# Cross-attention layer, four times in sequence: split-weight places from five to four, ring places from eleven to twelve, and a new table of the order of steps

## The reference, cut to what matters

```python
H = 1024; NH = 32; KVH = 8; HD = 32; GROUPS = 4; EPS = 1e-06     # 8 batches, L = S = 512
q = hidden_state @ Wq + bq                       # 512 x 1024
k = encoder_hidden_state @ Wk + bk               # 512 x 256
v = encoder_hidden_state @ Wv + bv               # 512 x 256
scores = jnp.einsum('bkgld,bksd->bkgls', q, k) * scale
scores = scores + encoder_attention_mask[:, :, None, :, :]
attn = jax.nn.softmax(scores, axis=-1)
out = jnp.einsum('bkgls,bksd->bkgld', attn, v)
out = out.transpose(0, 3, 1, 2, 4).reshape(b, l, H)
out = out @ Wo + bo
x = out + hidden_state                           # then a layer norm over H, times gamma, plus beta
```

## Time and profile before

| | before |
|---|---|
| median of 3 runs | 1693.84 us |
| the profiled execution, its own time | 1699.61 us |
| its span, first to last instruction | 1697.8 us |
| mean granted TensorE clock | 0.979 |
| busy: PE / DVE / ACT / POOL | 94% / 85% / 81% / 55% |
| share of the chain that ended last: PE / DVE / ACT | 68% / 8% / 4% |
| HBM over the span | 194 GB/s |

### The profile page before, as it was taken

One profiled execution on the slowest core, in us unless ns is written; L12 is line 12 of the kernel. 1 busy time (PEld: TensorE's weight loads), 2 busy tenths in 40 slices (PEclk: granted clock), 3 DMA queues, 4 the chain that ended last, 5 costly groups with the idle time before them and its releaser, 6 DMA issues.

```text
span 1697.8 us, 38272 instructions
## 1 busy us (share of the span) xinstructions
PE 1594.9 (94%) x14048; PEld 1107.2 (65%) x14048; DVE 1447.2 (85%) x2773; ACT 1370.9 (81%) x3186; POOL 936.6 (55%) x731
## 2 busy tenths in 40 slices
PE   4798899999999999999999999999999999999986
PEld 3565566666667666676676675777666676667654
DVE  4578899889888988899888898888988899887986
ACT  4678788869888788878988789887898879887794
POOL 5335433437745458544766357653585536856383
PEclk9899999999999999999999999999999999999998
DMA  9878787558895589756887668865898548894332
GB/s 201 233 207 213 203 215 202 158 132 184 251 249 131 149 198 272 222 146 154 213 265 186 165 155 211 277 170 146 196 241 255 156 130 206 270 277 126 98 99 106
DMA packets 357435, 325.54 MB, mean 192 GB/s; under 512 B 145792, under 2 KB 248192, under 8 KB 357248
## 3 DMA queue, kind: packets, MB, share of 16 engines
q1 hardware_dynamic: 353472, 322.55, 71.4%
q10 hardware_dynamic: 3776, 0.54, 0.3%
HBM read 245.38 MB, written 83.89 MB: 194 GB/s over the span
## 4 chain that ended last, share of the span: by engine, by line
PE 68%; DVE 8%; ACT 4%; issue 3%; DMA 1%; SPq 0%; POOL 0%; DVEq 0%; ACTq 0%
PE bank L1881 38%; PE bank L1962 13%; PE bank L1942 10%; DVE probs L1768 3%; DVE turned_p L1784 3%; PE bank L1977 3%; ACT probs L1666 2%; PE bank L2002 1%; PE bank L1990 1%; PE bank L1918 1%; DMA w_raw<-in_L_xattn_Wo_dram 1%; DVE ring_raw L1731 1%; ACT pv_sb L1679 0%; ACT y_sb L1690 0%; ACT part L1656 0%
## 5 line engine op out<-in xcount | busy, mean ns | idle before, releaser
L1881 PE MATMUL bank<-ring_hi,w_sb 128*128 128x512 f32 x2368 | 793.3, 400 | 29.0 <-issue 19.4
L1666 ACT ACTIVATE probs<-probs,shift 128x512 f32<-128x512 f32 x1024 | 729.4, 717 | 55.7 <-DVE shift L1768 54.4
L1768 DVE CUSTOM_DVE_ANT_0 probs<-bank,mask_l 128x512 f32<-128x512 f32 x1024 | 652.6, 677 | 105.7 <-PE bank L1942 97.4
L1784 DVE STREAM_TRANSPOSE turned_p<-probs 128x2048 f32<-128x2048 f32 x256 | 588.3, 2301 | 63.8 <-ACT probs L1666 62.1
L1551 POOL TENSOR_TENSOR w_sb<-w_raw,w_sb 128x512 fp32r<-128x512 f32 x320 | 413.4, 1298 | 384.9 <-ACT w_sb L1623 384.8
L1881 PEld LDWEIGHTS bank<-ring_hi,w_sb 128*128 128x128 f32 x2368 | 446.7, 190 | 154.8 <-issue 47.6
L1881 PE MATMUL bank<-ring_lo,w_sb 128*128 128x512 f32 x1184 | 469.4, 396 | 0.0
L1942 PE MATMUL bank<-k_stack,q_stack 96*128 96x512 f32 x1024 | 346.6, 415 | 24.5 <-DVE shift L1768 17.8
L1962 PE MATMUL bank<-turned_p,v_all 32*32 32x512 f32 x8192 | 294.7, 614 | 13.1 <-issue 7.5
L1566 POOL TENSOR_TENSOR ring_lo<-ring_raw,ring_hi 128x512 fp32r<-128x512 f32 x168 | 215.3, 1292 | 127.4 <-ACT ring_hi L1635 126.9
L1942 PEld LDWEIGHTS bank<-k_stack,q_stack 96*128 96x128 f32 x1024 | 189.2, 191 | 142.5 <-DVE shift L1768 55.9
(11 more groups left out here) (75 smaller groups left out, 963.2 us busy)
## 6 DMA issues: line engine op xcount, KB each, us to landing
w_raw<-w_d SPq DMA_DIRECT2D x144, 256.0 KB, 4.2
q_stack<-q_hi_d SPq DMA_DIRECT2D x128, 256.0 KB, 4.6
w_raw<-in_L_xattn_Wo_dram SPq DMA_DIRECT2D x128, 256.0 KB, 3.2
q_hi_d<-part_hi SPq DMA_DIRECT2D x64, 256.0 KB, 3.4
q_lo_d<-part SPq DMA_DIRECT2D x64, 256.0 KB, 3.9
q_stack<-q_lo_d SPq DMA_DIRECT2D x64, 256.0 KB, 4.2
v_all<-v_d SPq DMA_DIRECT2D x256, 64.0 KB, 2.7
out_dram<-y_sb SPq DMA_DIRECT2D x32, 512.0 KB, 4.5
```

The costliest lines, as they stand in the source:

```text
L1666: nc.scalar.activation(probs[:, st % 2, h, :], probs[:, st % 2, h, :], ACT.Exp, scale=-1.0, bias=shift[:, g % 2, i:i + 1], accum_out=sums[ ...
L1768: nc.vector.tensor_tensor_reduce(out=probs[:, st % 2, h, :], in0=S_ps[h][:, :], in1=mask_l[:, lb, :], scale=-1.0, scalar=HIGHEST, op0=ALU. ...
L1784: nc.vector.transpose(turned_p[:, :, block_of(g, st) + g % 2, :, :].rearrange("p j h c -> p h j c"), probs[:, st % 2, :, :].rearrange("p h ...
L1881: mm = nc.tensor.matmul(C[c][:, :], w_sb[:, n_w, (1, 0, 0)[third], d % 4, :], (hi, lo, hi)[third], start=(n == 0), stop=(n == 23))
```

## The change

`SLOTS`, the ring's places, goes from 11 to 12, and `NW`, the places for split weights, from 5 to 4. A place of either kind takes 4 KB of a partition, so memory stays as it is. `BASE` and all of `PLACES` have new numbers; the kinds and the number of the steps, `WINDOWS` and every instruction stay. A program's row of the diff shows what such numbers look like, and says nothing more:

```diff
-BASE = {1: 242.38, 2: 449.20, 3: 658.37, 4: 866.32, 5: 1074.27, 6: 1282.22, 7: 1490.17}
+BASE = {1: 232.33, 2: 435.46, 3: 639.46, 4: 840.58, 5: 1043.23, 6: 1245.48, 7: 1448.77}
...
-        "w_load Q": (
-            (13.583, 17.803),
+        "w_load Q": (
+            (23.287, 24.722),
...
-    SLOTS = 11
-
-    NW = 5
+    SLOTS = 12
+
+    NW = 4
```

More of the change, by code:

```diff
@@ new lines @@
+        "stack": (52.701, 77.364, 82.777, 111.918, 118.414, 153.577, 168.308, 197.908),
+        "recip": (86.598, 105.703, 129.112, 161.423, 171.071, 205.345, 215.721, 243.462),
+        "spread": (82.601, 115.511, 130.837, 160.246, 188.712, 222.964, 233.336, 240.415),
+        "v_load": (77.927, 82.788, 99.049, 124.782, 134.392, 160.941, 198.988, 210.865),
+        "pv": (84.915, 104.601, 128.361, 152.454, 175.118, 206.271, 223.447, 242.512),
+        "sel": (98.413, 118.866, 138.384, 164.408, 188.823, 215.945, 232.746, 255.261),
@@ new lines @@
+        "stack": (-7.624, -1.643, 26.536, 48.796, 68.761, 99.923, 131.304, 151.496),
+        "recip": (31.518, 47.625, 78.796, 102.726, 128.085, 158.252, 186.293, 206.818),
+        "spread": (35.422, 57.631, 80.693, 113.542, 132.238, 160.887, 189.330, 227.207),
+        "v_load": (-6.866, 9.124, 38.540, 99.912, 118.772, 121.624, 132.067, 163.237),
+        "pv": (31.884, 54.240, 81.788, 108.642, 131.388, 158.071, 184.939, 214.112),
+        "sel": (41.978, 61.293, 93.426, 117.760, 142.342, 175.628, 196.607, 229.196),
@@ L335 @@
-            (124.600, 131.861),
-            (138.176, 141.865),
+            (121.440, 121.769),
+            (129.232, 131.315),
+            (133.504, 137.115),
+            (138.870, 139.649),
         ),
         "w_hi kv": (
-            (123.172, 126.717),
-            (128.039, 132.341),
-            (141.477, 141.695),
-            (142.923, 150.012),
+            (125.884, 131.312),
+            (139.404, 142.699),
+            (147.408, 149.127),
+            (149.973, 154.490),
         ),
@@ L455 @@
+            (115.128, 119.290),
         ),
         "w_lo o": (
[L457 to L468 removed]
@@ L469 @@
-        "y_turn o": (69.641, 75.364, 94.730, 98.243, 102.980, 121.031, 126.326, 147.526),
-        "y_add o": (69.834, 70.418, 95.831, 98.791, 105.535, 124.055, 125.542, 149.802),
+            (56.103, 58.322),
+            (59.365, 62.524),
+            (63.590, 67.809),
+            (68.275, 73.344),
+            (81.980, 94.906),
+            (96.311, 107.880),
+            (108.672, 113.553),
+            (114.829, 123.368),
+        ),
+        "keep o": (67.524, 69.082, 75.621, 99.384, 101.983, 108.629, 124.682, 129.382),
@@ L483 @@
+        "z o": (163.862, 172.267, 180.578, 192.550),
+        "zmul o": (168.287, 174.416, 182.202, 198.021),
+        "zadd o": (168.400, 175.129, 191.825, 202.615),
+        "z_store o": (179.416, 196.150, 203.685, 210.336),
+        "root o": 157.335,
+        "rstd o": 159.813,
     },
@@ new lines @@
+        "stack": (-8.336, 12.458, 29.717, 48.201, 71.870, 99.130, 113.984, 165.901),
+        "recip": (32.055, 55.672, 87.023, 107.441, 131.672, 167.705, 188.555, 220.575),
+        "spread": (35.468, 52.659, 88.011, 106.475, 136.216, 171.661, 189.595, 226.047),
+        "v_load": (-11.038, 30.571, 56.573, 87.481, 97.941, 145.501, 150.413, 179.039),
+        "pv": (31.314, 51.805, 83.449, 109.798, 131.278, 159.868, 184.703, 217.027),
+        "sel": (40.991, 61.440, 91.326, 117.961, 142.787, 175.534, 202.280, 226.585),
@@ L700 @@
-        "y_turn o": (67.814, 76.014, 96.223, 99.263, 104.986, 125.290, 127.080, 147.928),
-        "y_add o": (67.751, 69.246, 96.593, 99.064, 104.062, 124.045, 126.255, 148.109),
+            (50.720, 52.659),
+            (63.201, 76.127),
+            (79.797, 83.364),
+            (84.540, 85.279),
+            (88.523, 89.046),
+            (94.919, 100.495),
+            (107.440, 108.925),
+            (115.712, 116.664),
+        ),
+        "keep o": (71.408, 74.815, 76.133, 88.157, 97.863, 104.962, 121.056, 129.109),
@@ L708 @@
-        "z o": (172.873, 174.156, 174.775, 181.954),
-        "zmul o": (180.075, 193.586, 196.132, 198.965),
-        "zadd o": (185.089, 199.833, 201.121, 212.459),
-        "z_store o": (195.130, 201.181, 205.726, 209.124),
-        "root o": 153.734,
-        "rstd o": 161.794,
+            (99.471, 103.601, 106.177, 109.064),
+            (152.681, 152.712, 154.416, 155.452),
+        ),
+        "res o": (19.516, 20.556, 34.801, 53.288),
+        "aggr o": (153.070, 155.944, 157.095, 157.232),
@@ L714 @@
+        "z o": (165.910, 173.278, 180.557, 193.182),
+        "zmul o": (169.868, 186.701, 188.100, 190.943),
+        "zadd o": (171.650, 188.474, 189.367, 203.143),
+        "z_store o": (176.211, 200.761, 206.660, 212.066),
+        "root o": 155.121,
+        "rstd o": 159.130,
     },
@@ L775 @@
-        "mask": (-15.884, -7.281, -1.566, -5.584),
[14 rows of a table removed]
-        ),
[2 rows of a table removed]
+            (36.333, 38.783, 40.181, 40.535),
+            (58.235, 58.582, 59.105, 60.390),
+            (87.341, 87.402, 90.312, 90.542),
+            (114.186, 115.176, 115.359, 115.389),
+            (135.630, 136.361, 137.599, 138.063),
+            (159.723, 160.270, 160.898, 161.291),
+            (182.621, 183.316, 184.498, 185.911),
+            (203.286, 205.977, 205.685, 205.735),
+        ),
+        "stack": (-9.716, 8.560, 30.313, 41.352, 75.159, 94.372, 138.733, 141.082),
@@ new lines @@
+        "recip": (26.017, 63.312, 86.147, 105.943, 125.853, 156.708, 178.007, 205.222),
+        "spread": (38.334, 61.960, 81.443, 100.607, 138.390, 166.349, 186.619, 195.931),
+        "v_load": (-12.772, 34.437, 50.974, 60.484, 94.383, 113.150, 170.071, 172.668),
+        "pv": (31.381, 53.330, 82.635, 112.499, 135.319, 155.228, 180.899, 199.826),
+        "sel": (42.923, 63.000, 96.248, 117.675, 139.040, 162.018, 187.127, 207.588),
+        "rbc": (44.097, 71.493, 96.419, 119.729, 139.116, 166.942, 189.235, 199.700),
@@ L927 @@
-        "res e": (-30.114, -26.465, 57.137, 57.836),
-        "z_store e": (219.999, 228.652, 229.634, 231.634),
[2 rows of a table added]
+        ),
+        "res o": (20.546, 24.885, 25.463, 64.595),
+        "aggr o": (148.017, 149.121, 148.558, 149.531),
+        "z o": (159.671, 165.117, 170.255, 177.028),
+        "zmul o": (157.017, 169.980, 175.510, 182.031),
+        "zadd o": (166.338, 170.524, 190.077, 205.623),
+        "z_store o": (177.515, 187.740, 197.414, 210.689),
+        "root o": 150.317,
+        "rstd o": 156.708,
```

675 lines of the change are left out of this document (305 added, 370 removed), and 556 rows, old and new, of the table PLACES.

## The result

| | before | changed |
|---|---|---|
| median | 1694.91 us (4 runs, 1692.93 to 1697.62) | 1676.09 us (4 runs, 1673.66 to 1678.15) |
| ratio | 1 | 0.9884, 95% interval 0.9864 to 0.9904 |
| the profiled execution, its own time / span | 1699.61 / 1697.8 us | 1676.28 / 1673.9 us |
| mean granted TensorE clock | 0.979 | 0.986 |

The account below looks back on a forecast made before the run. PE, busy 94% of the span, was taken as the bound, so only waits could change: -5.0 - 1.5 - 4.5 + 1.0 + 2.8 = -7.2 us, from 1693.8 to 1686.6 us. Its own range was 1680 to 1692, the whole range 1667 to 1706.

Parts of the forecast that it names:

- The square root in group 5: Batches 2 to 6, PE's wait after pv of group 5: copies 0.3 us earlier each, -1.5 us; bounds -11 and +4.
- Batches 2 and 4: ACT's queue no longer stopped by a late o0 weight transfer, so they fall to the others' time: -5.0 us.
- Prologue and batch 0: Prologue +1.0 us (weight cover, first scores); batch 0 -4.5 us: stack wait of group 1 -2.5, wait before its pv -2.0.
- Four places in the steady batches: Four weight places instead of five: refills stay covered while landing is under 7.5 us, cost 0.
- End: Row blocks and last pv: refills with four places come late, 1.4 to 1.5 and 1.3 us, together +2.8 us.
- Slower, places too few: Rival: one tight half in each of batches 1 to 6 meets a late landing, 1704.2 us; chance 0.22.
- Nothing comes of it: Rival: the waits trade places, what PE or ACT save in one group returns in the next, 1693.8 us; chance 0.2.
- More than forecast: Rival: batch 0's two waits (7.1) and five batches' wait behind pv (10.8) go entirely, plus 5.0: 1670.9 us; chance 0.13.

Follow-up runs that it names:

- run 2: Changed kernel with the keep of kv2 put back ahead of the first exponential of group 6 (table reload), batches 2 to 6: 1693.83 us, ratio 0.9986.
- Run 5: Kernel before with the first exponential of group 6 moved ahead of the keep of kv2, batches 2 to 6: 1687.75 us, ratio 0.9951.
- run 6: Kernel before with the first two copies of pv of group 5 moved 1.2 us sooner on ACT, batches 2 to 6: 1692.69 us, ratio 0.9975.
- run 8: Kernel before, first exponential of group 6 ahead of the keep of kv2, two roundings ahead of the keep of kv1: 1684.25 us, ratio 0.9942.
- run 9: As run 8, plus X2's transpose behind the last aggregate on DVE and its rounding behind the keep of kv2: 1683.44 us, ratio 0.9940.
- run 1: The changed kernel measured again, nothing edited: 1677.29 us, ratio 0.9896 to the kernel before.
- run 7: Changed kernel, first copies of pv of group 5 0.5 us sooner; in batch 0 group 1's stack loads ahead of half of q4's weights: 1681.06 us, 0.9910.
- run 10: Changed kernel with the rounding of the first half of kv3's weights moved ahead of the keep of kv1: 1676.18 us, ratio 0.9889.
- run 12: Kernel before, rounding of the second half of o0's weights moved behind the keeps of q6 and q7, batches 2 to 6: 1700.20 us, ratio 1.0018.

## Why the prediction was right or wrong

**The square root in group 5, -1.5 us: this step failed.** It carried the right mechanism and a tenth of its size. Group 6 gave 4.0 us a batch, 20 in the profiles (17.7 without the two scores that moved out), where the term had 1.5 in all; the one step of run 2 is worth 15.1 by the profiles and 16.5 by the medians. The working set one added rounding against one idle time, 1.0 - 0.6, as if the root stood where it stood before. But in the new order the root also comes earlier against PE: less of ACT's work lies between the keeps of kv1 and kv2 (two roundings and an exponential ahead of the root where there were six roundings). The root starts 3.7 us after the keep of kv1 instead of 5.1. So both table loads fit into time that ACT had, and the full 1.28 us left the path; the copies come 1.6 us sooner behind pv, not 0.4. Run 5 has the same step in the old order without this, and pays 1.0 us ahead of pv. Second, the clock: the text named it ("up to 3 us a batch come back") and left it out of the sum. By the length of group 6 it costs 0.8 to 0.9 us in three of the five batches before, 2.2 in batch 2, where the window has 0.59, nothing in batch 6, and 1.3 to 1.6 where it happens in run 2. A bound of -11 stood in the text, and even that was short.

**Batches 2 and 4, -5.0 us: right size, wrong cause.** They fell 2.2 us more than batches 3, 5 and 6, 4.4 in all. But more than half of batch 2's excess lay in group 6 (28.4 us against 26.2 to 27.1 in the others), behind the wait of the term above, and not at a transfer. And which batch meets a late transfer changes: group 1 takes over 21.5 us in batches 2 and 4 of the first profile, in 2 and 6 of run 6, in 2 of run 8, in 4 of run 9 and in none of run 5; with the new order it does so once, in batch 2 of run 2. Groups 1 to 3, which hold 51 scores in either order, average 396.6 us over the five batches in the five profiles with the old order (before, runs 5, 6, 8, 9) and 391.8 in the five with the new one (changed, runs 1, 2, 7, 10), 4.8 less. ACT's order, on which the term rested, gives none of it by itself (run 12 has 399.8). SP's order is the likelier cause; it was not tried alone. The text also took 2.9 us twice from one execution and set them against a median; that execution was 5.8 us above the median, as much as these two, so part of the term may never have been in the median. That the size came out is partly luck.

**Prologue and batch 0, +1.0 - 4.5 us: the sum about right, the parts not.** Six profiles with the old order reach pv of group 7 in batch 0 at 252.7 us in the mean (250.6 to 253.8), five with the new at 250.0 (248.6 to 251.3): -2.7 for the -3.5 forecast. The wait for the stack, meant to shrink by 2.5, grew from 4.26 to 5.50: SP issues there without a break from 57.3 us on, so that the last DMA of the stack leaves at 75.61 and not near 72. The wait ahead of pv of group 1 fell from 2.84 to 0.47, as forecast. That the sum came near is partly luck.

**Four places in the steady batches, 0: right.** No wait of PE's matmuls for weights shows in them. **End, +2.8 us: too much.** The stretch behind the last pv takes 31.5 us for 31.2. The late blocks are there, but as a wait of 0.82 us ahead of the last pv and one of 0.27 behind it, for the 1.4 and 1.3 of the working:

```profile
1639.69 0.47 PE L1918 MATMUL bank<-w_sb,ring_hi 128*128 128x512 f32 x1 [0.82 <-POOL w_sb L1551]
```

**The rivals.** "Slower, places too few" did not come, and neither did "Nothing comes of it": batches 2 to 6 take 198 to 199 us. "More than forecast" gave 1670.9 us, nearer to 1676.1 than the forecast, and its 10.8 us from the wait behind pv were the right place, though too small; its 7.1 from batch 0 were not, and its sum is near by luck.

**What is left open.** With the scores that moved taken out, groups 0, 3, 4, 5 and 7 change by no more than 0.3 us a batch. Groups 1 and 2 gain 0.3 and 1.0, with SP's order as a possible cause that was not tried alone, and 0.6 of the gain of group 6 beyond run 8 has no run that explains it. Nor does any run say what the twelfth place is worth in an order planned for eleven with the reload moved, beyond runs 8 and 9, which come to within 7 to 8 us of the changed kernel.

## What to carry to other kernels

A load of ACT's function table belongs in time in which ACT waits anyway. To price such a move, find what ACT waits for on both sides of it and write out ACT's queue from there to the step for which PE waits; do not net one idle time against one instruction. Size a term on waits that repeat in every batch, take late transfers by their mean over executions. Before two orders are compared stretch by stretch, count the instructions in each stretch. And when an experiment that removes a resource also reorders, run the new order with the resource as well.

## What the runs showed of the hardware

The same wait need not give the same clock. In run 2 PE waits 2.91 us at the same instruction in five batches; the clock falls to 0.79 or 0.81 of full speed over the window, that is to the lower of its two levels in part of it, in three and stays at 1.00 in two. Behind the five waits of 2.16 us of the kernel before it falls four times (0.59, and 0.79 three times) and stays at 1.00 once. In run 12 it falls behind two of the five waits of 2.16 us at that place, and another wait, of 2.12 us, ends at 916.71 and leaves it at 1.00:

```profile
911.00:919.00 8.00, 5.88 (x93) 3.72 (x77) 4.76 (x9) 7.09 (x16) 5.95 (x6) 1.00 0.72 217
...
916.00:924.00 8.00, 7.29 (x34) 5.08 (x35) 5.49 (x12) 7.43 (x18) 6.86 (x7) 1.00 0.54 160
```

And PE can stop inside a run of 128 matmuls without any semaphore, at the same instruction in five profiles with the new order (1.11 to 2.54 us, batch 1, group 3). In the first of them the 16 DMA engines were busy for nearly all of the time from 316.5 to 324.5 us, and the stall began at 323.4. The profile has a DMA queue of its own that it calls "instruction". In the first profile it moves one packet of 16 KB there, from 323.55 to 324.73 us; the view of 323 to 325 us counts it so:

```profile
q8 instruction: 1, 0.02, 3.7%
```

All five profiles have such a packet at this place, and in all five PE goes on 1.2 to 1.6 us after it has landed. So instructions that come late are a likely cause, beside the other transfers; it was not tried.
